# Scan stage of a hybrid layer: the four lane products of a section, split two and two between VectorE and GpSimd

## What is computed

```python
def _combine(left, right, W):                  # LANES = 4, hd = 32
    q = left.reshape(B, T, LANES, hd)
    k = right.reshape(B, T, LANES, hd)
    v = ((left + right) @ W).reshape(B, T, LANES, hd)
    scores = einsum('btld,btmd->btlm', q, k) * hd ** (-0.5)
    att = softmax(scores, axis=-1)
    z = einsum('btlm,btmd->btld', att, v)
    z = _rms_norm(z) / denom                   # denom = 1, 2, 3, 4 by lane
    return left + z.reshape(B, T, C)

def _pscan2(x, W, identity):
    d = 1
    while d < T:                               # 11 steps for T = 2048
        shifted = concatenate([ident, x[:, :-d]], axis=1)
        x = _combine(shifted, x, W)
        d *= 2
    return x
```

## Time and profile before

| | |
|---|---|
| median of 3 runs | 2170.57 (2169.71 to 2172.13) |
| profiled execution | 2170.21 |
| its span in the trace | 2168.5 |
| mean granted TensorE clock | 0.93 |
| PE (TensorE) busy | 1837.5, 85% of the span |
| DVE (VectorE) busy | 1445.8, 67% |
| ACT (ScalarE) busy | 976.7, 45% |
| POOL (GpSimd) busy | 686.8, 32% |

### The profile page before, as it was taken

How to read it: one execution, slowest core, us unless ns; L and a number is a source line. 1 busy time by engine, 2 the same in 40 slices (tenths; PEclk the granted TensorE clock), 3 DMA queues, 4 the chain that set the end, 5 groups by cost and what they waited for, 6 DMA issues and landing times. The chain is left out here.

```text
span 2168.5 us, 41226 instructions
## 1 busy us (share of the span) xinstructions
PE 1837.5 (85%) x12999; PEld 1200.2 (55%) x13126; DVE 1445.8 (67%) x3077; ACT 976.7 (45%) x2157; POOL 686.8 (32%) x492
## 2 busy tenths in 40 slices
PE   5599999999999999999997193799999999994474
PEld 3144444444444444444445183798888888884363
DVE  6877777777777777776754233588888888884322
ACT  4166666666666666666664021233333333332220
POOL 4300000000000000000001543477777777773442
PEclk9699999999999999999997596899999999997587
DMA  3200000000000000000003423222222222221623
GB/s 110 72 13 17 10 13 16 11 13 16 8 16 15 8 15 14 10 16 15 8 1 130 148 62 95 78 78 78 78 77 86 79 85 79 77 58 59 205 68 97
DMA packets 171549, 115.79 MB, mean 53 GB/s; under 512 B 10934, under 2 KB 161846, under 8 KB 171196
## 3 DMA queue, kind: packets, MB, share of 16 engines
q1 hardware_dynamic: 167356, 106.31, 16.8%
q0 software_dynamic: 4096, 8.46, 1.1%
HBM read 63.98 MB, written 50.72 MB: 53 GB/s over the span
## 5 line engine op out<-in xcount | busy, mean ns | idle before, releaser
L597 ACT ACTIVATE probs<-ps_s 128x512 f32<-128x512 f32 (+3 forms) x1280 | 604.2, 542 | 384.0 <-PE ps_s L636 164.7
L542 DVE TENSOR_REDUCE chunk_max<-ps_max 128x1 f32<-128x512 f32 x768 | 496.0, 684 | 84.8 <-PE ps_max L646 57.7
L646 PE MATMUL ps_max<-Ks,Qs 126*128 126x512 bf16 (+3 forms) x1280 | 455.7, 358 | 42.4 <-DVE chunk_max L542 21.2
L633 PE MATMUL ps_s<-Qs,Ks 128*128 128x512 bf16 (+3 forms) x1153 | 391.9, 348 | 1.6 <-ACT probs L597 1.3
L546 DVE CUSTOM_DVE_ANT_0 ps_max<-ps_max,mask 128x128 f32<-128x128 f32 (+3 forms) x512 | 249.1, 502 | 178.8 <-PE ps_max L646 178.6
L661 PE MATMUL ps_o<-probs,Vp 128*32 128x512 f32 (+3 forms) x2560 | 339.5, 558 | 1.5 <-ACT O_sb L580 1.1
L497 POOL TENSOR_TENSOR A_b<-A_newton,b_tile 128x128 f32<-128x128 f32 x32 | 14.6, 457 | 999.5 <-ACT A_newton L604 999.5
L1383 POOL TENSOR_TENSOR lane_products<-L,q 128x1024 f32<-128x1024 f32 x132 | 309.5, 2375 | 4.0 <-DMA L<-scanned 4.0
L633 PEld LDWEIGHTS ps_s<-Qs,Ks 128*128 128x128 bf16 x1280 | 133.4, 104 | 173.0 <-ACT probs L597 109.7
L646 PEld LDWEIGHTS ps_max<-Ks,Qs 126*128 126x128 bf16 x1280 | 124.9, 98 | 148.2 <-DVE chunk_max L542 41.1
L1438 DVE TENSOR_TENSOR weighted<-exp_scores,psV_s 128x4096 f32<-128x4096 f32 x44 | 194.1, 4411 | 0.0
(11 more groups left out here) (227 smaller groups left out, 2358.1 us busy)
## 6 DMA issues: line engine op xcount, KB each, us to landing
scanned<-q SPq DMA_DIRECT2D x44, 512.0 KB
L<-scanned SPq DMA_DIRECT2D x44, 512.0 KB
m_w<-in_L_ffn_w_dram SPq DMA_DIRECT2D x32, 512.0 KB
Qs<-q_parts SPq DMA_DIRECT2D x192, 32.0 KB
Ks<-k_parts SPq DMA_DIRECT2D x192, 32.0 KB
dispatched<-m_blank SPq DMA_DIRECT2D x2, 2080.0 KB
m_blank<-dispatched SPq DMA_DIRECT2D x16, 260.0 KB
routed<-m_blank SPq DMA_DIRECT2D x2, 2048.0 KB
```

The source lines that it names most:

```text
L542: nc.vector.tensor_reduce(out, scores[:], axis=AX.X, op=ALU.max).then_inc(max_reduced, 1)
L597: nc.scalar.activation(dst, ps_s[(k + r) % R][:, q0:], ACT.Exp, scale=SCALE).then_inc(exp_done, 1)
L633: last = nc.tensor.matmul(ps_s[(k + r) % R][:, q0:], K[r][:, kt * P:(kt + 1) * P], Q[r][:, g * QW + q0:(g + 1) * QW], start=True, stop=not ...
L646: nc.tensor.matmul(ps_max[(k + r) % R][:, 0:w], Q[r][0:MROW, i * P:(i + 1) * P], K[r][0:MROW, ck * QW:ck * QW + w], start=True, stop=True) ...
```

## The change

```diff
                     out = lane_products[ch % 2]
                     pool.wait_ge(l_loaded[ch], s * 16 + 16)
                     wait(pool, sT_in_psum, g - 1)
-                    lane_product(nc.gpsimd, ch, 1, out)
                     lane_product(nc.gpsimd, ch, 2, out)
                     lane_product(nc.gpsimd, ch, 3, out).then_inc(p_pool, 1)
...
                 if head:
                     dve.wait_ge(l_loaded[ch], s * 16 + 16)
                     wait(dve, sT_in_psum, g - 1)
-                    lane_product(nc.vector, ch, 0, lane_products[u]).then_inc(p_dve, 1)
+                    lane_product(nc.vector, ch, 0, lane_products[u])
+                    lane_product(nc.vector, ch, 1, lane_products[u]).then_inc(p_dve, 1)
```

## The result

The changed kernel takes 2186.65 us in the median of 4 runs (2185.29 to 2187.82), the kernel before 2170.43 (4 runs, 2169.71 to 2172.13). The ratio is 1.0073 with a 95% interval of 1.0056 to 1.0091: slower by 12 to 20 us. The forecast was 2186, range 2176 to 2200.

What follows compares the result with a forecast made beforehand. Scan sections were taken as bound by a score chain (12.40) and a port chain (13.76), mean step 13.07. 41 steps gave +16.0, the start -0.3: +15.7 on 2170.21 made 2185.9, stated as 2186, range 2176 to 2200.

Steps and rivals of the forecast that it cites:

- the scores': Scan chain from TensorE's score sum through best_score, weighted and value matmuls to the next score sum; 12.40, the short step.
- the port's: Scan chain through z_normed, GpSimd's products and total_sq, where two-SBUF-input VectorE and GpSimd instructions exclude each other; 13.76, the long step.
- P0: VectorE's old product in each scan section, right behind z_normed; 1.14 start to start, holding the port until z_normed's start + 2.36.
- S: Start of TensorE's score sum in a scan section; best_score forecast at S + 5.90, the next S at S + 13.46.
- The relief on GpSimd: Scan: one product fewer per section, 2.33; GpSimd's last product ends at z (z_normed's start) + 10.2, was 11.54; total_sq stall gone.
- P1's price: Scan: P1, the product added to VectorE behind P0, lasts 3.39 because GpSimd's add already waits; 1.14 with a free port.
- the alternating port: Scan: VectorE and GpSimd take turns, P0, add, P1, then two GpSimd products; the forecast case, chance 0.76.
- The step: Scan section length: 13.46 in every section instead of the mean 13.07, +0.39; over 41 steps +16.0.
- The start: First scan sections: one GpSimd product fewer ahead of the first score sum, value matmuls end nearly as late; -0.3.
- VectorE keeping the port: Scan rival: VectorE holds the port through P0 and P1, step 12.60, time 2149; chance 0.14.
- The mixture: Scan rival: P1 gets in ahead of the add in some sections, mean step near 13.03, time 2169; chance 0.06.
- TensorE's clock: Scan rival: granted clock falls, score sums slow by 1.08; 2230 if in every section, 2197 in a quarter; chance 0.04.

Runs made afterwards that it cites:

- The PSUM kernel: Changed kernel with VectorE's second product reading one input from PSUM instead of SBUF, in all sections but the first; 2138.71 us, ratio 0.985 to the kernel before.
- the one with P0 ahead and P1 late: Changed kernel with VectorE's first product moved ahead of z_normed and its second behind weighted; 2137.30 us, ratio 0.985 to the kernel before.
- the kernel with three products behind an unheld add: Kernel before, one product on VectorE and three on GpSimd, with VectorE's moved ahead of z_normed; 2159.33 us, ratio 0.9957.
- With P0 ahead: Changed kernel with only VectorE's first product and its two waits moved ahead of z_normed; 2162.33 us, ratio 0.9966 to the kernel before.
- with P1 late: Changed kernel with only VectorE's second product moved, from ahead of best_score to behind weighted; 2148.99 us, ratio 0.990 to the kernel before.

## Why the prediction was right

**What bounds the kernel.** Right. Two chains, the scores' (12.40) and the port's (13.76), took turns. The PSUM kernel and the one with P0 ahead and P1 late show the first alone, at 12.33 (there best_score comes 4.77 after S, not 4.86); the kernel with three products behind an unheld add shows the second still there.

**The relief on GpSimd.** Right: the products end at z + 10.2 (1600.22 to 1610.45), as worked out, and total_sq and with_eps are free again.

**P1's price.** Right, and it carried everything. I took the alternating port from the start of the scan and had 3.39; measured 3.40. The open point was whether VectorE keeps the port when nothing stands between its two instructions. It doesn't: 4.54, 7.84 and 6.81 for two, three and four of them. The start of the scan in the changed kernel shows the same, four VectorE products in 13.27 beside GpSimd's:

```profile
1375.44 13.27 DVE L1383 TENSOR_TENSOR lane_products<-L,q 128x1024 f32<-128x1024 f32 x4 [6.39 <-DMA L<-scanned]
1388.63 0.28 DVE L1428 TENSOR_REDUCE best_score<-psS 128x32 f32<-128x128 f32 x1
```

**The step.** Forecast 13.46, measured 13.50. Single steps are 13.46 and 13.54 in pairs; the longer ones have a wait of 0.45 instead of 0.38 for the exponential (the row of 1593.34 in the same timeline, against 1606.80) or 0.65 instead of 0.56 for rs. Across the 40 steps from section 3 on, against 13.08 instead of 13.07, that is 16.6 where I had 15.6.

**The start.** Missed by a little. -0.3 was forecast for it, and 0.39 for the step into section 3. best_score of section 1 starts 0.37 earlier, measured from the scan's first product (1375.44 to 1388.63, against 1376.18 to 1389.74). Two things undo that. best_score of section 2 comes 14.67 after it, where it came 13.95 before, 0.72 later. TensorE's value matmuls of that section, in the changed kernel:

```profile
1394.28 3.78 PE L1572 MATMUL psV_s<-S_pair,UT 128*128 128x128 f32 x16 [3.07 <-DVE weighted L1438]
```

They took 2.57 before. The mean granted clock from 1395 to 1400 is 0.57, against 0.68 before: here the clock cost something that I hadn't counted. And the step into section 3, which holds the first collision, is 13.47 against 12.33, since the kernel before had a short step there and not its mean: 1.14 more. So best_score of section 3 is 1.5 later where I had 0.1.

The scan as a whole, from GpSimd's first product to its first instruction of the stage behind, is 18.0 longer (1375.41 to 1987.39, against 1376.15 to 1970.15); I had 15.7. The profiled executions differ by only 15.1, as the other stages, in which nothing is changed, were 2.9 shorter in the second. The medians differ by 16.2. So the hit within 1 us has luck in it: errors of mine of one sign, 2.3 together, and a difference between executions of the other.

**The rivals.** VectorE keeping the port: out, as above. The mixture: out, every section has the same phase. TensorE's clock: 1.00 from 1400 to 1940, so not in the steps; it acted once, in section 2, for the 0.7 above.

**What I had overlooked** did no harm here but would have in the next change: the transfer loop. I wrote that the load was in time, which was so; I had no row for when it lands, and took the store's length for it.

## What to carry to other kernels

When work moves to the faster of two engines that exclude each other on a port, don't price it by its free duration or by the busy shares: list who is waiting at the moment it asks. In these runs two such instructions back to back gave the other engine its turn in between, so each can cost a whole instruction of the other. Put one of them where the other engine is idle or waits for something else: here the same split went from 0.7% slower to 1.5% faster. Before moving a consumer forward, find a row that shows when its input lands; a transfer that nobody has waited for yet has no visible length.

## What the runs showed of the hardware

- A VectorE instruction with two SBUF inputs that is queued directly behind another doesn't keep the port from a waiting GpSimd one. Handing over costs nothing to speak of: P1 ends 1.09 after the add, where a free one takes 1.14 from start to start.
- With one input in PSUM the same multiply of 128 x 1024 isn't held: 1.22 beside a running add.
- With P0 ahead, a load of 512 KB was used 4.04 after its issue (1600.18 to 1604.22; 3.80 to 4.33 in the sections from 1420 to 1920, median 3.95), where the store of the same size had let the next instruction go after 3.20 (1596.98 to 1600.18). Why the load takes longer these runs don't tell.
- The score sum of 32 matmuls takes 3.83 in the kernel before and 3.74 to 3.76 in most of the others, at the same granted clock; with P1 late, and in one and three with the one ahead, it takes 3.87 and 3.83. What makes the difference is left open.
